# A graph-network kernel on one core: order of the first operations of the count loop, of four loads, and of the first products of x and W0

## The reference, cut to what matters

```python
h = x @ W + b
adj = jnp.zeros((N, N)).at[row, col].set(1.0)
adj = adj.at[col, row].set(1.0) + jnp.eye(N)
adj = adj / jnp.maximum(adj.sum(axis=1, keepdims=True), 1.0)
out = diffusion_weights[0] * h
cur = h
for i in range(3):
    cur = adj @ cur
    out = out + diffusion_weights[i + 1] * cur
return jax.nn.relu(out)
```

## Time and profile before

| | |
|---|---|
| median of 3 runs | 385.28 us (385.11 to 385.52) |
| profiled execution, its own time | 384.96 us |
| its span, first to last instruction | 383.1 us |
| PE busy | 368.6 us, 96% of the span |
| DVE busy | 277.6 us, 72% |
| ACT busy | 235.3 us, 61% |
| granted TensorE clock, mean | 0.991 of full |

### The profile page before, as it was taken

How to read it: one execution, slowest core, us unless ns; L and a number is a source line. 1 busy time by engine, 2 the same in 40 slices (tenths; PEclk the granted TensorE clock), 3 DMA queues, 4 the chain that set the end, 5 groups by cost and what they waited for, 6 DMA issues and landing times.

```text
span 383.1 us, 7752 instructions
## 1 busy us (share of the span) xinstructions
PE 368.6 (96%) x2740; PEld 217.2 (57%) x2740; DVE 277.6 (72%) x615; ACT 235.3 (61%) x402; POOL 100.5 (26%) x91
## 2 busy tenths in 40 slices
PE   8799999999999999999999999999999999999980
PEld 3355585444444444444444444444568889999980
DVE  7799988469976772226755445553995879999994
ACT  8999867678512444222651111478877999999235
POOL 3003000099700477001990000466300000121210
PEclk9999999999999999999999999999999999999996
DMA  5970050032000000000442000133203113110006
GB/s 167 385 234 0 3 204 18 2 124 95 2 0 0 1 2 3 0 2 1 88 91 41 0 0 2 28 79 75 41 0 115 56 55 113 56 57 3 2 3 222
DMA packets 27974, 22.70 MB, mean 59 GB/s; under 512 B 19552, under 2 KB 20768, under 8 KB 27936
## 3 DMA queue, kind: packets, MB, share of 16 engines
q1 hardware_dynamic: 27072, 19.06, 16.8%
q10 hardware_dynamic: 864, 3.15, 2.3%
HBM read 15.87 MB, written 2.13 MB: 47 GB/s over the span
## 4 chain that ended last, share of the span: by engine, by line
PE 88%; DVE 5%; ACT 4%; issue 2%; DVEq 0%; POOL 0%; POOLq 0%
PE ps L807 22%; PE ps L1212 10%; PE ps L1153 8%; PE ps L1054 7%; PE ps L1095 7%; PE ps L1017 7%; PE ps L1008 7%; PE ps L854 6%; PE ps L998 4%; PE ps L983 4%; PE ps L875 3%; ACT cts L518 2%; PE ps L930 1%; PE ps L895 1%; DVE early L1791 1%
## 5 line engine op out<-in xcount | busy, mean ns | idle before, releaser
L807 PE MATMUL ps<-big,xTs 128*128 128x512 f16 x384 | 84.3, 379 | 0.0
L807 PEld LDWEIGHTS ps<-big,xTs 128*128 128x128 f16 (+1 forms) x384 | 37.0, 98 | 43.4
L715 ACT ACTIVATE big<-big,uvt 128x1024 bf16<-128x1024 f32 x55 | 58.9, 1146 | 0.0
L616 ACT ACTIVATE big<-xcur,nmr,rstd (+1 forms) x24 | 19.5, 814 | 33.5 <-DVE nmr L1507 33.5
L447 POOL TENSOR_TENSOR big<-xcur,big x16 | 18.5, 1156 | 60.1 <-ACT xcur L617 59.2
L854 PE MATMUL ps<-big,xTs 128*128 128x512 f32 x64 | 32.6, 606 | 0.0
L464 POOL TENSOR_TENSOR xcur<-xcur,c 128x512 f32<-128x512 f32 (+2 forms) x8 | 8.9, 1107 | 88.1 <-DVE c L1710 83.4
L486 ACT ACTIVATE big<-ps 128x512 f16<-128x512 f32 (+1 forms) x16 | 9.4, 587 | 33.3 <-PE ps L807 30.9
L1153 PE MATMUL ps<-big,cst 128*128 128x260 f16 x256 | 29.8, 275 | 0.0
L1017 PE MATMUL ps<-big,adj 128*128 128x512 f16 x128 | 27.9, 379 | 0.0
L1054 PE MATMUL ps<-cst,big 128*128 128x512 f16 x128 | 27.8, 379 | 0.1
(11 more groups left out here) (233 smaller groups left out, 713.3 us busy)
## 6 DMA issues: line engine op xcount, KB each, us to landing
big<-u_rows ACTq DMA_DIRECT2D x6, 512.0 KB, 3.6
xcur<-in_x SPq DMA_DIRECT2D x1, 2048.0 KB, 16.9
out<-xcur SPq DMA_DIRECT2D x8, 256.0 KB, 2.3
big<-in_W SPq DMA_DIRECT2D x1, 1024.0 KB, 5.9
xTs<-in_xT SPq DMA_DIRECT2D x1, 1024.0 KB, 10.0
big<-in_W3T SPq DMA_DIRECT2D x1, 1024.0 KB, 12.6
xTs<-in_W1T SPq DMA_DIRECT2D x1, 1024.0 KB, 5.3
xTs<-in_wc SPq DMA_DIRECT2D x1, 1024.0 KB, 8.2
```

The lines of the kernel that those rows point to most:

```text
L715: act.activation(above[:, a % AHEAD, :], uf[:, h % 2], ACT.Relu, scale=BIG, bias=vb[:, j, h:h + 1]).then_inc(S["above_in"], 1)
L807: return mm(bank, lhs(k)[a], rhs(k)[b], start=start and k == 0 and n == 0, stop=stop and k == KT - 1 and n == 2)
```

## The change

- The loads of x and W0 move ahead of the diffusion weights: xT's first 128 nodes (256 KB) first, then W0 in two halves of 512 KB with a semaphore each, the second piece of xT, then `dwb`, then the third piece.
- One `h` part follows each of quads 0 to 3 (`H_FIRST = KT`), and the other 28 are spread over quads 4 to 28. The three zero matmuls after quad 0 and after quad 1 are gone. The waits for x and W0 move from "after quad 2" into `h_part`.
- ACT: the first one-hot (`lo_hots(0)`) comes right after `distances(0)`, with neither the wait for `dwb` nor a fill of zeros between; the tile that this fill wrote goes to POOL, whose fill is two tiles. The wait for `dwb` stands ahead of the first `h_upper`. `constants()` is split: the two iota extensions (line 537) keep their place, and the copies to `id16` and `sel` go behind the last `h_upper` of the loop.
- PSUM banks of the transposes and zero matmuls change (2, 3, 4 to 4, 5, 3), because `h` now uses bank 2 early. A semaphore near the end of the program is merged with another.

```diff
-H_FROM = 2
+H_FIRST, H_FROM = KT, 4
-WARM = (9, 3, 6, 3)
+WARM = (9, 3, 6)
-ZERO_ACT, ZERO_POOL = 5, 6
+ZERO_ACT, ZERO_POOL = 4, 6
...
         def h_parts(q):
+            if q < H_FIRST:
+                return (q,)
+
             def upto(i):
-                return NT * KT * sum(27 + window(j) for j in range(H_FROM, i)) // sum(
+                return H_FIRST + (NT * KT - H_FIRST) * sum(27 + window(j) for j in range(H_FROM, i)) // sum(
                     27 + window(j) for j in range(H_FROM, H_TO))
...
-            sp.dma_start(dwb[:], dw...).then_inc(S["dw_in"], 16)
-            sp.dma_start(w0raw, W0...).then_inc(S["w_in0"], 16)
-            for i, (n0, n1) in enumerate(XT_NODES):
+            sp.dma_start(xT32[:, :, 0:P], xT...[:, :, 0:P]).then_inc(S["xT_in0"], 16)
+            for k in range(0, KT, 2):
+                sp.dma_start(w0raw[:, k:k + 2, :], W0...[:, k:k + 2, :]).then_inc(S[f"w_in0_{k}"], 16)
+            for i, (n0, n1) in enumerate(XT_NODES[1:], 1):
+                if i == 2:
+                    sp.dma_start(dwb[:], dw...).then_inc(S["dw_in"], 16)
...
             tiles_up = 0
-            act.wait_ge(S["dw_in"], 16)
             distances(0)
-            zeros(2 * F_LO_AFTER, ZERO_ACT)
+            lo_hots(0)
+            distances(1)
             for i, q in enumerate(mine):
-                if i + 1 < len(mine):
+                if 0 < i < len(mine) - 1:
                     distances(i + 1)
-                lo_hots(i)
+                if i:
+                    lo_hots(i)
                 if i == 2:
-                    constants()
+                    keys_late()
...
                 if tiles_up < NT - 1 and h_quad(tiles_up) + 3 <= q:
+                    if tiles_up == 0:
+                        act.wait_ge(S["dw_in"], 16)
                     h_upper(tiles_up)
                     tiles_up += 1
             for t in range(tiles_up, NT - 1):
                 h_upper(t)
+
+            constants()
...
             def h_part(t, k):
+                if k == 0 and t == 0:
+                    pe.wait_ge(S["xT_in0"], 16)
+                if k % 2 == 0 and t == 0:
+                    pe.wait_ge(S[f"w_in0_{k}"], 16)
...
                 quad(q)
-                if q < H_FROM:
-                    warm(WARM[3])
-                if q == H_FROM:
-                    pe.wait_ge(S["key_in"], 1)
-                    pe.wait_ge(S["nslo_in"], 2)
-                    pe.wait_ge(S["xT_in0"], 16)
-                    pe.wait_ge(S["w_in0"], 16)
...
-            dve.wait_ge(S["c32z"], 5)
+            dve.wait_ge(S["c32z"], 4)
```

More of the change, by code:

```diff
@@ L310, in h_parts @@
         def h_parts(q):
+            if q < H_FIRST:
+                return (q,)
             def upto(i):
-                return NT * KT * sum(27 + window(j) for j in range(H_FROM, i)) // sum(
+                return H_FIRST + (NT * KT - H_FIRST) * sum(27 + window(j) for j in range(H_FROM, i)) // sum(
                     27 + window(j) for j in range(H_FROM, H_TO))
-            return range(upto(q), upto(q + 1)) if H_FROM <= q < H_TO else ()
+            return tuple(range(upto(q), upto(q + 1))) if H_FROM <= q < H_TO else ()
         def h_quad(t):
@@ L333, in _ @@
                          allow_slow_non_contiguous=True).then_inc(S["edges"], 16)
-            sp.dma_start(dwb[:], dw.rearrange("(a d) -> a d", a=1).broadcast_to([P, STEPS + 1])).then_inc(S["dw_in"], 16)
-            sp.dma_start(w0raw, W0.rearrange("(k p) n -> p k n", p=P)).then_inc(S["w_in0"], 16)
-            for i, (n0, n1) in enumerate(XT_NODES):
+            sp.dma_start(xT32[:, :, 0:P], xT.rearrange("(k p) n -> p k n", p=P)[:, :, 0:P]).then_inc(S["xT_in0"], 16)
+            for k in range(0, KT, 2):
+                sp.dma_start(w0raw[:, k:k + 2, :], W0.rearrange("(k p) n -> p k n", p=P)[:, k:k + 2, :]).then_inc(S[f"w_in0_{k}"], 16)
+            for i, (n0, n1) in enumerate(XT_NODES[1:], 1):
+                if i == 2:
+                    sp.dma_start(dwb[:], dw.rearrange("(a d) -> a d", a=1).broadcast_to([P, STEPS + 1])).then_inc(S["dw_in"], 16)
                 sp.dma_start(xT32[:, :, n0:n1], xT.rearrange("(k p) n -> p k n", p=P)[:, :, n0:n1]).then_inc(S[f"xT_in{i}"], 16)
@@ L498, in _ @@
             copy(f_lo, i_lo).then_inc(S["f_lo_in"], 1)
-            zeros(F_LO_AFTER, 2 * F_LO_AFTER)
+            zeros(F_LO_AFTER, ZERO_ACT)
             def split_hi(n, name, raw):
@@ L507, in _ @@
             act.wait_ge(S["tr"], 1)
-            act.activation(lo16[:], by_chunk(ps[:, 2, 0:E // P]), ACT.Copy, bias=1.0).then_inc(S["nslo_in"], 1)
-            copy(nslo[:], by_chunk(ps[:, 2, 0:E // P]), -1.0).then_inc(S["nslo_in"], 1)
+            act.activation(lo16[:], by_chunk(ps[:, 4, 0:E // P]), ACT.Copy, bias=1.0).then_inc(S["nslo_in"], 1)
+            copy(nslo[:], by_chunk(ps[:, 4, 0:E // P]), -1.0).then_inc(S["nslo_in"], 1)
             act.wait_ge(S["nslo_in"], 2)
@@ L532, in h_upper, with keys_late, constants @@
                 copy(acc[:, t, :], ps[:, h_bank(t), :], dwb[:, 0:1]).then_inc(S["acc0"], 1)
-            def constants():
+            def keys_late():
                 for k0, k1 in ((KEYS0, 2 * KEYS0), (2 * KEYS0, KEYS)):
                     act.activation(iota_rep[:, k0:k1, :], iota_rep[:, 0:k1 - k0, :], ACT.Copy, bias=float(k0)).then_inc(S["keys_late"], 1)
+            def constants():
                 copy(id16[:], id32[:]).then_inc(S["const16"], 1)
@@ L819, in warm @@
                 for _ in range(n):
-                    mm(ps[:, 4, :], blank[:, 0:P], blank, start=True, stop=True)
+                    mm(ps[:, 3, :], blank[:, 0:P], blank, start=True, stop=True)
             pe.wait_ge(S["blank_in"], 1)
@@ L826, in _ @@
             for c in range(NC):
-                ins = pe.transpose(ps[:, 2, c * NG:(c + 1) * NG], f_lo[:, c * P:(c + 1) * P], id32[0:NG, 0:NG])
+                ins = pe.transpose(ps[:, 4, c * NG:(c + 1) * NG], f_lo[:, c * P:(c + 1) * P], id32[0:NG, 0:NG])
             ins.then_inc(S["tr"], 1)
@@ L831, in _ @@
             for c in range(NC):
-                ins = pe.transpose(ps[:, 3, c * NG:(c + 1) * NG], f_key[:, c * P:(c + 1) * P], id32[0:NG, 0:NG])
+                ins = pe.transpose(ps[:, 5, c * NG:(c + 1) * NG], f_key[:, c * P:(c + 1) * P], id32[0:NG, 0:NG])
             ins.then_inc(S["tr"], 1)
@@ L882, in far_columns @@
             def far_columns():
+                pe.wait_ge(S["nslo_in"], 2)
+                pe.wait_ge(S["key_in"], 1)
                 pe.wait_ge(S["idx_far"], 2)
@@ L1177, in _ @@
                 if j == 3:
-                    pe.wait_ge(S["lim_in"], 1)
+                    pe.wait_ge(S["lim_a"], 4)
                     pe.transpose(ps[0:1, 3, P:2 * P], lim[:, 3:4], id32[:]).then_inc(S["lim_done"], 1)
@@ L1338, in _ @@
             dve.wait_ge(S["tr"], 2)
-            dve.tensor_copy(key16[:], by_chunk(ps[:, 3, 0:E // P])).then_inc(S["key_in"], 1)
+            dve.tensor_copy(key16[:], by_chunk(ps[:, 5, 0:E // P])).then_inc(S["key_in"], 1)
             dve.wait_ge(S["first_in"], 5)
@@ L1653, in _ @@
             dve.wait_ge(S["lim_a"], 3)
-            stt(lim[:, 3:4], lim[:, 1:2], VMAX * BIG, lim[:, 3:4], ALU.is_le, ALU.mult).then_inc(S["lim_in"], 1)
+            stt(lim[:, 3:4], lim[:, 1:2], VMAX * BIG, lim[:, 3:4], ALU.is_le, ALU.mult).then_inc(S["lim_a"], 1)
             y_lower(NT - 2)
```

## The result

The changed kernel is slower: 387.97 us median of 6 runs (387.49 to 389.41) against 385.29 (385.11 to 385.52), ratio 1.0073 (95% interval 1.0058 to 1.0087). The profiled execution took 387.67 us, 2.7 more than the 384.96 of before. Yet the count loop did become faster.

The account below looks back on a forecast made before the run. PE was taken to bound the kernel, losing time only at the count loop's start: 1.15 + 1.8 = 2.95 us, less 0.4 waiting for DVE, gives 2.55; median 385.28 to 382.7 us, range 382.0 to 384.1.

Parts of the forecast that it names:

- so the profiled execution goes from 384.96 to 382.4: End of the sum: the count loop's gain of 2.55 us is carried unchanged to the kernel's end.
- move nothing on the path: PSUM banks, merged semaphore and one wait less on DVE: claimed to have no effect on the critical path.
- The working of the loop: Count loop: PE gains 1.15 us from ACT and 1.8 from earlier h parts, less 0.4 waiting for DVE.
- the one-hot of quad 8: ACT's line up to quad 8: this one-hot comes 0.95 + 1.25 - 1.05 = 1.15 us earlier.
- The loads: Start of the loop: W0's halves land by 8.5 and 10.0 us; waits up to 1.0 us cost 0.
- Quad 20: Count loop: first place where PE, running ahead, must wait for DVE, 0.4 us.
- The step: First diffusion step after the count loop: begins at 55.0 us instead of 57.57.
- The gain: Whole kernel: 2.55 us, from 2.95 on PE less 0.4 of waiting for DVE.
- POOL's rival: Start: POOL's longer fill delays DVE's i_lo and ACT by 0.94 us; gain 1.6, time 383.7 us; chance 0.12.
- DVE's start at 4.14: Sign for POOL's fill holding up DVE: DVE starts on the keys just when that fill ends, 4.19 us.
- PE ahead of quad 8: PE's work before quad 8 ends at 16.4 us, leaving a wait of about 1.0 us for ACT as slack.
- The clock's rival: Before quad 8, TensorE's clock falls without zero matmuls; six h parts at 1.2 GHz give 388.2 us; chance 0.04.

Follow-up runs that it names:

- e4: Changed kernel with 12 PE instructions put back as met waits and POOL's fill split, its second tile only after DVE's keys are done: 383.05 us, ratio 0.9945.
- e9: Changed kernel with POOL's fill split and eight zero matmuls instead of six in the last group before quad 0, no waits: 382.69 us, ratio 0.9936.
- e1: Changed kernel with 12 PE instructions put back as 24 already met waits: 384.14 us, ratio 0.9967.
- e2: Kernel before with only its six zero matmuls behind quads 0 and 1 left out: 390.4 us, ratio 1.0128.
- e10: Changed kernel with POOL's fill split and 240 never-executed instructions in PE's branch for far edges: 388.9 us, ratio 1.0104.
- e5: Changed kernel with POOL's fill split and no PE instructions put back: 387.15 us, ratio 1.005.
- e6: Changed kernel with POOL's fill split and 2 PE instructions (4 met waits) put back: 387.43 us, ratio 1.0059.
- e8: Changed kernel with POOL's fill split, two more zero matmuls before quad 0 and 16 met waits: 382.86 us, ratio 0.9938.
- e7: Changed kernel with POOL's fill split and 4 PE instructions (8 met waits) put back: 382.95 us, ratio 0.9936.

## Why the prediction was wrong

**The step that failed** is the last of the working: "so the profiled execution goes from 384.96 to 382.4". It carried the gain at 55 us to the end, and it priced the six zero matmuls by their time alone. They also hold 12 places in PE's program, and with them gone a jump 86 us behind the first step lands three instructions ahead of an edge. Price 4.22 us, more than the whole gain. That the banks, the merged semaphore and one wait less on DVE "move nothing on the path" fits the rows, but no run has them alone.

**The working of the loop** was right once that and POOL's fill are out of the way. ACT: the one-hot of quad 8 was forecast 1.15 us earlier; in e4 it starts at 16.82 against 17.88, 1.06. The loads: no part of `h` waits for one. Quad 20: 0.4 us of waiting for DVE was forecast, and in e4 its four matmuls last 0.82 us against 0.56, 0.26 more. These two misses of about 0.1 us have opposite signs, so the end of the sum comes out closer than its terms. The step: 55.0 forecast, 55.03 in e4. The gain: 2.55 forecast, 385.28 - 382.69 = 2.6 in e9.

**POOL's rival** (0.12) came true inside the loop: 0.73 us on `i_lo`, step at 55.70 instead of 55.03. It priced the delay of ACT at 0.94, measured 0.77, and its own time of 383.7 is near e1's 384.14, which also holds a late clock. DVE's start at 4.14 beside the fill's end at 4.19 was no sign of it: with the longer fill DVE still starts on the keys at 4.12, and only the operation behind that is held. The rule of the Trainium skill named there (SBUF, "SBUF: two separate sides") fits these rows, though none shows in which mode a DVE operation runs. Held were a tensor_scalar of 256 columns, one of 21 and a copy. A tensor_tensor (line 1347 of e4, 6.37 us) and a reduction (line 1349, 6.50 us) ran beside the second fill at their usual 0.20 and 0.40 us, and a tensor_scalar of one column (line 1328 of the changed kernel, 4.12 us) took 0.14 us beside the first.

**PE ahead of quad 8** was mis-sized: 16.4 and a wait of 1.0 us, measured a wait of 0.27 (with ACT 0.77 late) and none in e4. In e4 the first part of `h` starts at 8.73 and not at 8.25, since the second fill holds DVE; PE waits another 0.25 for the far columns (line 1421 of the changed kernel); and the quads and transposes take 0.4 more than the 1.7 allowed. So the slack of 1.0 us was not there: in e4 ACT's one-hot ends at 17.44 and quad 8 starts at 17.50, behind PE's own work. That this cost no more than 0.1 us was luck.

**The clock's rival** did not come true in the loop, where real work took the zeros' place. The clock fell behind the hole. That its 388.2 us is near the measured 387.97 is chance: 2.52 of the 4.22 us lost are the hole, which it doesn't have. e2 shows the fall in the loop, where nothing took the zeros' place.

**What stays open.** The Trainium skill (Runtime: NRT & Kernel Launch, "Instruction fetch mechanics") says that code is fetched ahead in sequence in blocks of 16 KiB, 256 instructions, and that a taken branch out of the window of two such blocks has to wait for its target. The packets of 16384 bytes and e10's step of 256 agree. The wait does not: here a jump to a target 545 instructions away costs 0.1 to 0.5 us when it lands past the edge. When it lands ahead of it, the piece it lands in runs, and it takes 3.0 us from the branch (141.08 to 144.14, 145.29 to 148.26; 3.9 in e2's profiled run) until the piece behind the edge can. Nor is landing past an edge free everywhere: e10's jump over the far edges lands at instruction 874, three past an edge if they come every 256 (871), and cost 3.05 us. Which pieces PE has at hand when it jumps, no run here tells.

## What to carry to other kernels

An edit that changes the number of instructions on an engine moves every later branch of that engine against the edges of its code. When a change is slower than its parts, look for a new wait behind a branch, far from the edit: "issue", or an engine's name whose work had long been done or runs on time. Put the same number of instructions back before judging the idea. Zero matmuls do three things: they take time, they hold the clock, and they take up place; price all three. A fill on POOL is not free beside DVE: look in the trace at which DVE operations it would overlap, and compare their durations with and without it.

## What the runs showed of the hardware that I had not expected

- Stalls of 2.4 to 3.1 us behind a taken branch (the changed kernel, e5, e6, e10) are followed by 3 to 4 us at the lower clock, in e2 by nearly 7. That added 1.7 us in the changed kernel. A hole of 0.72 us (e10) and a gap of 1.02 us left the clock up.
- The beginning differs between the profiled runs: the 3 zero matmuls behind the first transposes took 0.82 us (after, e4, e5, e8) or 1.46 us (e1, e6, e7), in no order of the number of waits put back. The trace's record of the granted clock begins at 4.1 to 4.7 us in the first four and at 6.9 to 10.3 in the other three, and the zero matmuls of 0.43 us lie before that begin; the clock's column reads 1.00 there too.
